# Decoder layer, self-attention: band mask added to the scores by an identity matmul in place of GpSimd's product behind the exponentials

## What is computed

```python
def _dilated_mask(N):
    diff = j - i
    return (jnp.abs(diff) <= K_WIN * DILATION) & (jnp.mod(diff, DILATION) == 0)    # 8, 2

q = q / (norm(q) + 1e-6); k = k / (norm(k) + 1e-6)       # per head, 32 wide
scores = jnp.einsum('bhnd,bhmd->bhnm', q, k)
scores = jnp.where(allowed[None, None], scores, -jnp.inf)
attn = jax.nn.softmax(scores, axis=-1)
out = jnp.einsum('bhnm,bhmd->bhnd', attn, v)             # then out @ out_w.T + out_b
```

## Time and profile before

| what | value |
|---|---|
| median of 3 runs | 1330.51 us |
| the profiled execution | 1330.41 us, of it the span 1328.4 us |
| main block's loop over units on TensorE | from 66.7 to 398.8 us of the span |
| TensorE busy over the whole span | 1242.1 us (93%) |
| GpSimd busy over the whole span | 235.1 us (18%), nearly all in the attention |
| mean granted clock of TensorE | 0.974 of 2.4 GHz |

### The profile page before, as it was taken

How to read it: one execution, slowest core, us unless ns; L and a number is a source line. 1 busy time by engine, 2 the same in 40 slices (tenths; PEclk the granted TensorE clock), 3 DMA queues, 4 the chain that set the end, 5 groups by cost and what they waited for, 6 DMA issues and landing times.

```text
span 1328.4 us, 17214 instructions
## 1 busy us (share of the span) xinstructions
PE 1242.1 (93%) x6888; PEld 1000.8 (75%) x6888; DVE 576.7 (43%) x1046; ACT 417.9 (31%) x756; POOL 235.1 (18%) x230
## 2 busy tenths in 40 slices
PE   6789889999984789999999999999999999999997
PEld 4567667677763668888878888887788888888886
DVE  4556677675753363233346233325444123123211
ACT  4244444445352343222335222224332111111111
POOL 0145656645664000000000000000000000000000
PEclk9899999999987889999999999999999999999999
DMA  6200010201022362100043100132330100000000
GB/s 238 64 23 11 5 61 1 72 33 34 31 96 94 102 225 64 32 24 32 32 132 107 32 24 30 34 118 65 104 95 32 32 0 32 32 0 26 7 1 32
DMA packets 47765, 73.31 MB, mean 55 GB/s; under 512 B 4177, under 2 KB 16465, under 8 KB 47697
## 3 DMA queue, kind: packets, MB, share of 16 engines
q1 hardware_dynamic: 44432, 66.08, 15.1%
q10 hardware_dynamic: 3264, 6.29, 1.7%
HBM read 55.58 MB, written 16.78 MB: 54 GB/s over the span
## 4 chain that ended last, share of the span: by engine, by line
PE 56%; issue 4%; DVE 3%; DMA 2%; ACT 1%; POOL 0%; SPq 0%; DVEq 0%; ACTq 0%; POOLq 0%
PE score L66 10%; PE score L68 10%; PE score L67 10%; PE work L66 8%; PE work L68 7%; PE work L67 7%; PE work L1485 2%; DMA x_stage<-in_ctx_n 1%; PE work L1457 1%; DVE cn_l L1335 1%; ACT x_pr L1260 0%; DMA x_q_raw<-qp_scratch 0%; PE work L1494 0%; PE score L1803 0%; DVE fxn L1735 0%
## 5 line engine op out<-in xcount | busy, mean ns | idle before, releaser
L66 PE MATMUL score<-fxt_h,w_hl 128*128 128x512 f32 x384 | 149.8, 390 | 0.8 <-DVE fxt_l L1740 0.8
L68 PE MATMUL score<-fxt_h,w_hl 128*128 128x512 f32 x384 | 149.6, 390 | 0.0
L67 PE MATMUL score<-fxt_l,w_hl 128*128 128x512 f32 x384 | 149.5, 389 | 0.0
L1760 DVE SCALAR_TENSOR_TENSOR hid<-score,gate 128x512 f32<-128x512 f32 x48 | 33.2, 691 | 236.6 <-ACT gate L1689 236.6
L1414 DVE TENSOR_TENSOR pt_l<-work,pt_h 128x512 fp32r<-128x512 f32 x64 | 44.0, 690 | 183.3 <-ACT pt_h L1300 183.3
L1689 ACT ACTIVATE gate<-score 128x512 f32<-128x512 f32 x48 | 28.7, 598 | 266.0 <-PE score L68 265.9
L66 PE MATMUL score<-ct_h,x_q_h 128*128 128x512 f32 x256 | 104.3, 408 | 2.6 <-ACT x_pr L1260 2.6
L66 PE MATMUL work<-cn_h,pt_h 128*128 128x512 f32 x256 | 103.0, 402 | 0.0
L493 POOL TENSOR_TENSOR probs<-probs,band 128x544 f32<-128x544 f32 (+1 forms) x64 | 89.8, 1404 | 71.4 <-ACT probs L613 71.1
L68 PE MATMUL score<-ct_h,x_q_l 128*128 128x512 f32 x256 | 101.8, 398 | 0.0
L67 PE MATMUL score<-ct_l,x_q_h 128*128 128x512 f32 x256 | 101.5, 396 | 0.0
(11 more groups left out here) (182 smaller groups left out, 2534.4 us busy)
## 6 DMA issues: line engine op xcount, KB each, us to landing
x_stage<-in_ctx_n SPq DMA_DIRECT2D x16, 512.0 KB, 4.6
x_stage<-in_ctx_n ACTq DMA_DIRECT2D x12, 512.0 KB, 3.6
x_in<-in_x SPq DMA_DIRECT2D x16, 256.0 KB, 2.7
xs<-in_x SPq DMA_DIRECT2D x4, 1024.0 KB, 5.1
x_scratch<-xs SPq DMA_DIRECT2D x4, 1024.0 KB, 4.4
qp_scratch<-xs SPq DMA_DIRECT2D x4, 1024.0 KB, 4.3
x_q_raw<-qp_scratch SPq DMA_DIRECT2D x16, 256.0 KB, 2.7
xr<-x_scratch SPq DMA_DIRECT2D x16, 256.0 KB, 2.6
```

The lines of the kernel that those rows point to most:

```text
L66: pe.matmul(out, hi_s, hi_m, start=first, stop=False)
L67: pe.matmul(out, hi_s, lo_m, start=False, stop=False)
L68: return pe.matmul(out, lo_s, hi_m, start=False, stop=last)
L1760: V.scalar_tensor_tensor(hid[:], score[:, 2 * (f % 2) + 1, :], WSCALE, gate[:, f % 2, :], ALU.mult, ALU.mult).then_inc(hid_done, 1)
```

## The change

The band becomes a bias: 0 inside, -32768 outside (`OUTSIDE`). It is built in the setup block by the same GpSimd instructions, in memory that only that block uses; ScalarE copies it and the identity to fp32r tiles `mbias` and `ident_r` at the very start of its program, behind a wait for GpSimd's constants. In `scores`, two matmuls of the identity (all 128 rows) with the bias pattern, repeated for two heads, open the accumulation of each of the two banks; the six matmuls follow and add to it. `mask` and `p_ready` are gone, `weighted` waits for `exp_done`. `nb1` and `nb2` become halves of one tile. All else stays as it was, the order on each engine too.

```diff
@@ constants, setup block
+OUTSIDE = -32768.0
-    band = sb("band", [P, WIN])
+    mbias = sb("mbias", [P, WIN], F32R)
+    ident_r = sb("ident_r", [P, P], F32R)
+    band = over.put("band", [P, WIN])
-            nc.gpsimd.memset(band[:], 1.0).then_inc(consts, 1)
+            nc.gpsimd.memset(band[:], 0.0).then_inc(consts, 1)
-            nc.gpsimd.affine_select(out=band[:], in_=band[:], compare_op=ALU.is_ge, fill=0.0,
+            nc.gpsimd.affine_select(out=band[:], in_=band[:], compare_op=ALU.is_ge, fill=OUTSIDE,
...
         @block.scalar
         def _(act):
+            act.wait_ge(consts, 8 + HPG)
+            nc.scalar.copy(mbias[:], band[:])
+            nc.scalar.copy(ident_r[:], ident[:])
             for src, hi, lo, n in sets[:2]:
@@ main block
-    nb1, nb2 = sb("nb1", [P, ST]), sb("nb2", [P, ST])
+    nb = sb("nb", [P, 2, ST])
+    nb1, nb2 = nb[:, 0, :], nb[:, 1, :]
@@ GpSimd
-            def mask(s, n):
-                lo, w, c0 = window(n % ST)
-                pool.wait_ge(exp_done, s * UN + n + 1)
-                PL.tensor_tensor(probs[:, n % 2, :, 0:w], probs[:, n % 2, :, 0:w],
-                                 band[:, c0:c0 + w].unsqueeze(1).to_broadcast([P, HPG, w]),
-                                 ALU.mult).then_inc(p_ready, 1)
...
-                    if n not in LATE:
-                        mask(s, n + 1)
...
-                    if n == 7:
-                        mask(s, 8)
...
-                    if n == 15 and more:
-                        mask(s + 1, 0)
@@ TensorE, scores
-                for kt, qt, first_mm, last_mm in ((kt_h, qbd_h, True, False), (kt_h, qbd_l, False, False),
+                for a in range(2):
+                    PE.matmul(out[a], ident_r[:], mbias[:, c0:c0 + w].unsqueeze(1).to_broadcast([P, 2, w]),
+                              start=True, stop=False)
+                for kt, qt, first_mm, last_mm in ((kt_h, qbd_h, False, False), (kt_h, qbd_l, False, False),
                                                   (kt_l, qbd_h, False, True)):
@@ TensorE, weighted
-                pe.wait_ge(p_ready, s * UN + n + 1)
+                pe.wait_ge(exp_done, s * UN + n + 1)
```

More of the change, by code:

```diff
@@ L402, in attention_phase @@
     exp_done = sem("exp_done")
-    p_ready = sem("p_ready")
     pv_done = sem("pv_done")
@@ L517, in _ @@
             scale_units(0, 1)
-            mask(0, 0)
             for s in range(NS):
```

## The result

The changed kernel takes 1338.17 us (median of 4 runs, 1336.37 to 1338.96) against 1330.44 us before: ratio 1.0052, 95% interval 1.0035 to 1.0070. It is slower by 0.4 to 0.5%, where the prediction said 1335 us and 0.3%. The profiled execution is 1337.71 us with a span of 1335.9 us, 7.5 us more than before.

A forecast was written before the change was run, and what follows sets the result against it. The loop was taken to run at TensorE's pace. Added matmuls 26.9 us, less 15.8 of stalls and 6.6 of half-clock time, gave +4.5 us on 1330.41: 1335 us, 0.3% slower, range 1325 to 1347.

The forecast's parts named there:

- What bounds the kernel: Loop over units, 66.6 to 398.8 us: TensorE busy 308.9 of 332.2 us, so added TensorE instructions cost full price.
- the 26.9 us of matmuls: TensorE in the loop: two identity matmuls in each of 63 units, 55 at 0.455 us and 8 at 0.24.
- the 6.6 us of clock: Half-clock stretches behind the stalls at 100.41, 136.46, 173.64 and 381.97 go: 4.9 us for three, 1.7 for the last.
- Price of a unit: Identity matmuls ahead of a unit's scores: 0.24 us for the first, 0.22 for the second, 0.46 together.
- the one in which the identity's load is free: Rival, chance 0.08: the identity's load overlaps the weighted sums, a unit costs 0.345 us, total 1329 us.
- the one in which its change of shape is: Rival, chance 0.13: the identity pays only its streaming, 0.25 us a unit, 15.8 us in all, total 1324 us.
- The mask on VectorE: Inverse-norm steps no longer held by GpSimd's mask; TensorE stalls shrink by 15.8 us, including both of 2.48 us.
- the two head stalls: TensorE's waits ahead of `heads`, 2.89 us at 100.41 and 3.44 at 136.46: both gone.
- The stalls before the output projection at step 7: TensorE stalls of 0.89 us at 183.18 and 1.12 one sequence later: no mask touches them, each loses 0.45.
- the one at 381.97: TensorE stall of 2.32 us in the last sequence: three units between take 1.36 off, leaving 0.96.
- Setup and the loop's end: ScalarE's two setup copies hidden behind a DMA; TensorE's direct wait of 1.59 us at 401.49 goes, valued at nothing.
- The rival in which only TensorE's own added work shrinks the waits: Chance 0.22: stalls lose only 9.0 us, half-clock stretches stay, so +17.9 us, 1348 us.

The follow-up runs named there:

- the doubled pair: The changed kernel with each pair of identity matmuls issued twice: 1353.39 us, ratio 1.0150.
- the moved pair: The changed kernel with a unit's identity matmuls issued ahead of the weighted sums, behind the full-array projection, for 55 of 64 units: 1329.83 us, ratio 0.9967.

## Why the prediction was right, and where its terms were off

*What bounds the kernel.* Right: the loop runs at TensorE's pace. TensorE's busy time rose by 20.3 us, as much as the 26.9 us of matmuls less the 6.6 us of clock. That the clock's part agrees is luck, as said below. The spans differ by 7.5 us where the sum had 4.5. Of the 3.0 us between them 1.2 are stalls that stayed in the loop, 0.65 lie ahead of it and 1.1 behind it.

*Price of a unit.* I forecast 0.46 us at a unit of 288 columns (0.455 on average) and measured 0.47, and its two parts stand. The streaming, 0.26, is that of the doubled pair. The change of shape, 0.20, is what the moved pair wins in a unit without waits (4.64 to 4.45 us). All 54 moved pairs, at 0.20 us each, would win 10.8 us; measured on different chips, the gain was 7 to 8 us by the medians and 10 to 11 by the ratios. Two rivals fall with this, the one in which the identity's load is free and the one in which its change of shape is: had either been so, moving the pair would have won less or nothing. By the rule of the Trainium skill on loads pulled ahead (TensorE: Matmul & The Clock Gate, Part 2) the time would have been 1329. Within one shape the runs agree with it: in the kernel before, a projection's load starts at 89.18 for a matmul that starts at 89.41. Across shapes they don't: in the changed kernel a load of the identity starts at 195.25, its matmul at 195.26.

*The mask on VectorE.* Right: the two head stalls and the two of 2.48 us went, and the run without a mask left the 0.5 and 1.2 us that the held steps explain. Of 15.8 us of stalls to go, 14.6 went (21.45 - 6.84). Two terms were off. The stalls before the output projection at step 7 both kept 0.68 us, where I had 0.44 and 0.67. And the one at 381.97 was to shrink to 0.96 and is 2.41.

*Why that one stayed* is the term that I mis-sized, together with the clock. In the last sequence TensorE waits at 373.15 and again at 381.97 for a chain that runs on without it. Before, the stretch between began at half clock; now it is at full clock, and what TensorE wins it waits (windows as in the earlier trace rows, first before, then after):

```profile
373.10:376.50 3.40, 3.35 (x34) 2.35 (x38) 3.32 (x9) 2.41 (x5) 2.77 (x4) 0.51 0.62 238
```

```profile
378.30:382.50 4.20, 4.17 (x54) 2.91 (x55) 4.12 (x10) 3.68 (x7) 0.00 (x0) 1.00 0.40 156
387.00:390.40 3.40, 3.40 (x28) 2.25 (x28) 2.64 (x7) 2.01 (x4) 0.21 (x1) 0.54 0.00 0
```

From the one wait's end to the other's it is 8.82 us before and 8.67 after, whatever the clock. In the repeated run of the changed kernel a half-clock stretch did fall there, and the wait was 0.98 us, about what I had said; from wait to wait it took 8.66 us:

```profile
379.40:382.80 3.40, 3.40 (x27) 2.43 (x28) 3.32 (x10) 2.02 (x4) 0.00 (x0) 0.51 0.48 184
388.10:391.50 3.40, 3.40 (x33) 2.49 (x34) 2.84 (x7) 2.57 (x5) 0.17 (x1) 1.00 0.00 0
```

I had counted four stretches as gone, behind 100.41, 136.46, 173.64 and 381.97. In the first profiled execution of the changed kernel the first three went. So did the one behind 373.15, which gave nothing, because TensorE waited the time away. The fourth stayed, at 0.54 from 387.0 on, and cost the 1.7 us that I had booked as won. Four stretches went as forecast, but not the same four, and that is why the busy time agrees.

*Setup and the loop's end.* Right: the copies are hidden, the wait of 1.59 us was worth nothing. The loop starts 0.65 us later, but that differs between executions: the first heads come at 67.32 us in the changed kernel, at 66.47 in its repeated run, and at 67.57 in the run without a mask, whose setup is that of the kernel before. The clock at the first units differs between executions as well. In the changed kernel it was 0.84 on average from 68.8 to 79.2 us, in its repeated run 0.51. The 1.1 us behind the loop lie on unchanged code, and what made them is not shown.

*The rival in which only TensorE's own added work shrinks the waits* (1348 us) falls by the run with no mask. The run with identity and a full-length GpSimd operation is that rival made real, and took 1344.55. Its stalls fell by 9.7 us where the rival had 9.0; its 17.9 us were too many because it kept all the half-clock stretches, and shorter stalls dropped two of them.

## What to carry to other kernels

Work moved from an idle engine to the one that bounds the loop costs its full price, and it pays only if it buys waits that this added work would not have closed by itself: here a cost of 12 to 14 us and a gain of 14 to 17, each measured alone, came out as a loss of 5 to 8. Look for the few places where the cheap engine's work gets in the way, and move only those: ten units of 64, with shorter GpSimd instructions in the others, were enough for the whole gain. A piece added to TensorE belongs beside work of the same array shape: the pair cost 0.24 us there and 0.47 elsewhere.

## What was not expected of the hardware

An affine_select with a single input holds VectorE's small steps as a product of two tensors does, up to that instruction's end: a step of 0.23 us took 0.59 to 0.74. GpSimd's elementwise operation on 576 columns took 1.43 us with the second operand read in full, 1.15 us with the second operand a single repeated column, and one affine_select 0.70 us.
